# Attention's second pass: causal masks as POOL selects on the exponentials in place of mask matmuls

## The reference

```python
x_proj = x @ Wqkv + bqkv
q = x_proj[:, :, :C].reshape(B, n_head, T, hd)      # n_head 16, hd 16
k = x_proj[:, :, C:2 * C].reshape(B, n_head, T, hd)
v = x_proj[:, :, 2 * C:].reshape(B, n_head, T, hd)
att = jnp.einsum('bhtd,bhsd->bhts', q, k) * (1.0 / jnp.sqrt(jnp.float32(hd)))
causal = jnp.tril(jnp.ones((T, T), dtype=bool))
att = jnp.where(causal, att, jnp.float32(-jnp.inf))
att = jax.nn.softmax(att, axis=-1)
y = att @ v
y = jnp.transpose(y, (0, 2, 1, 3)).reshape(B, T, C)
return y @ Wproj + bproj
```

## Time and profile before

| | us |
|---|---|
| three runs | 4186.95, 4191.31, 4209.79 (median 4191.31) |
| profiled execution | 4200.33 |
| its span, first to last instruction | 4198.4 |
| PE busy in the span | 3853.1 (92%) |
| DVE busy | 2985.4 (71%) |
| ACT busy | 2260.1 (54%) |
| POOL busy | 1380.0 (33%) |

### The profile page before, as it was taken

How to read it: one execution, slowest core, us unless ns; L and a number is a source line. 1 busy time by engine, 2 the same in 40 slices (tenths; PEclk the granted TensorE clock), 3 DMA queues, 4 the chain that set the end, 5 groups by cost and what they waited for, 6 DMA issues and landing times. The chain is left out here.

```text
span 4198.4 us, 81224 instructions
## 1 busy us (share of the span) xinstructions
PE 3853.1 (92%) x28814; PEld 2524.3 (60%) x28814; DVE 2985.4 (71%) x7504; ACT 2260.1 (54%) x4454; POOL 1380.0 (33%) x1724
## 2 busy tenths in 40 slices
PE   4997899997579999999999999999999996899997
PEld 4886666664345555555555555555555553667664
DVE  6997457575467777777777777777777773467575
ACT  0110466664156656666666666666666664465664
POOL 2332133332524334243333334334343320132332
PEclk8999899999689999999999999999999998899999
DMA  1332112111767677766767766777676741112111
GB/s 57 100 100 94 42 46 65 52 56 38 136 93 116 104 99 112 106 109 100 120 99 107 118 103 105 107 117 102 101 117 99 107 67 47 41 57 64 41 56 46
DMA packets 701475, 361.54 MB, mean 86 GB/s; under 512 B 305072, under 2 KB 668080, under 8 KB 701104
## 3 DMA queue, kind: packets, MB, share of 16 engines
q1 hardware_dynamic: 701104, 356.65, 47.2%
HBM read 204.49 MB, written 150.99 MB: 85 GB/s over the span
## 5 line engine op out<-in xcount | busy, mean ns | idle before, releaser
L1591 DVE TENSOR_REDUCE att_maxima<-att_s 128x1 f32<-128x512 f32 (+3 forms) x3072 | 1521.6, 549 | 434.0 <-PE att_s L1770 217.2
L1691 ACT ACTIVATE att_probs<-att_s 128x512 f32<-128x512 f32 (+1 forms) x2560 | 1330.6, 556 | 869.9 <-PE att_s L1770 511.5
L1824 PE MATMUL att_s<-att_qs,att_ks 49*128 49x512 f32 (+3 forms) x3072 | 999.2, 401 | 89.6 <-DVE att_maxima L1591 42.2
L1800 PE MATMUL att_s<-att_ks,att_qs 48*128 48x512 f32 (+3 forms) x3072 | 993.6, 408 | 20.9 <-POOL att_ks L1464 13.4
L1824 PEld LDWEIGHTS att_s<-att_qs,att_ks 49*128 49x128 f32 x3072 | 473.9, 186 | 647.5 <-ACT att_probs L1691 403.4
L1852 PE MATMUL att_o_ps<-att_probs,att_vs 128*32 128x512 f32 (+3 forms) x6144 | 632.8, 498 | 1.9 <-issue 1.1
L1770 PE MATMUL att_s<-att_mask,att_places 64*128 64x64 bf16 (+1 forms) x5632 | 590.9, 209 | 0.6 <-issue 0.6
L1800 PEld LDWEIGHTS att_s<-att_ks,att_qs 48*128 48x128 f32 x3072 | 502.3, 188 | 36.2 <-issue 16.5
L1057 PE MATMUL ffn_h2p<-ffn_h,ffn_w 128*128 128x512 f32 x768 | 366.2, 599 | 2.8 <-ACT ffn_h L938 0.7
L1770 PEld LDWEIGHTS att_s<-att_mask,att_places 64*128 64x128 bf16 x5632 | 284.1, 96 | 112.4 <-issue 43.3
L1509 POOL TENSOR_TENSOR att_x_res<-att_x_res,att_bp_row 128x512 f32<-128x512 f32 x64 | 81.3, 1283 | 748.2 <-DMA att_x_res<-x 746.7
(11 more groups left out here) (238 smaller groups left out, 5809.3 us busy)
## 6 DMA issues: line engine op xcount, KB each, us to landing
att_staged<-qk_scratch SPq DMA_DIRECT2D x768, 128.0 KB, 7.1
qk_scratch<-att_parts SPq DMA_DIRECT2D x128, 512.0 KB, 3.1
ffn_x<-x SPq DMA_DIRECT2D x64, 512.0 KB, 5.2
ssm_x<-in_L_attn_a_x_dram SPq DMA_DIRECT2D x32, 512.0 KB, 3.9
x<-ssm_y SPq DMA_DIRECT2D x32, 512.0 KB, 2.9
x<-ffn_y SPq DMA_DIRECT2D x32, 512.0 KB, 3.1
att_x<-x SPq DMA_DIRECT2D x32, 512.0 KB, 12.7
v_scratch<-att_v_tok SPq DMA_DIRECT2D x32, 512.0 KB, 3.4
```

The lines of the kernel that those rows point to most:

```text
L1591: last = v.tensor_reduce(maxima_of[p][:, g, blk, 1 if t0 else 0:2 if t0 else 1], s1_ps[(2 * unit + 1 - g) % 3][:, col:col + w], AX.X, ALU.max)
L1691: a(probs[u % 2][2 * g + p][:, 0:n], bank[:, 0:n], ACT.Exp).then_inc(exp_done, 1)
L1800: last = mm(bank[:, col:col + w], rows_of(qs[buf], g, KROWS, p, BT * blk, BT * (blk + 1)), rows_of(ks[buf], g, KROWS, p, t0, t1), start=k ...
L1824: last = mm(bank[:, col:col + w], rows_of(ks[buf], g, SHIFT + 1, p, BT * j, BT * (j + 1)), rows_of(qs[buf], g, SHIFT + 1, p, t0, t1), star ...
```

## The change

The second pass's scores are no longer masked by matmuls. After the exponentials of a step of a unit with diagonal blocks POOL sets what lies under the diagonal to zero by `affine_select`, in place in `probs`, for both row groups in one instruction (so `probs` becomes one tile of 128 x 4 x 512 per unit parity). A new semaphore `cut` counts these steps; `times_v` of these six units waits for it behind its wait for the exponentials. The first pass's masks stay. POOL's other tasks move: the four casts from step 10 to 7, 8.6, 9.9 and 11.2 one by one, the two biases from 4 to 6, the normalisation from one piece at 8 to its powers and first quarter at 13 and further quarters at 14.7, 15.7 and 16.7. The selects stand at 2u + p + 0.5. The carrier instruction in `normalise` goes.

```diff
@@ -1170,11 +1170,13 @@
              [(0, 32, 64)], [(1, 32, 64)], [(2, 32, 64)], [(3, 32, 64)], [(4, 32, 64)],
              [(5, 40, 64), (7, 56, 64)], [(6, 48, 64)]]
     FIRST_U2, LAST_U2 = (0, 3), (2, 9)
+    ON_DIAGONAL = [u for u, unit in enumerate(PASS2) if any(t0 == BT * j for j, t0, _ in unit)]
     UNITS1, UNITS2 = 2 * len(PASS1), len(PASS2)
     STEPS = 2 * UNITS2
     LEAD = 4
     EVACUATE_AT = (7, 1)
-    LAY_OUT_AT, PREPARE_AT, PIECES = 10, 6, 2
+    LAY_OUT_AT, PREPARE_AT, PIECES = (7, 8.6, 9.9, 11.2), 6, 2
+    BIAS_AT, NORMALISE_AT = 6, (13, 14.7, 15.7, 16.7)
 
     X_PROLOGUE = 22
 
@@ -1228,7 +1230,7 @@
         qs = [sb(f"qs{k}", [P, HD * QT], F32R) for k in range(4)]
         ks = [sb(f"ks{k}", [P, HD * QT], F32R) for k in range(4)]
         vs = [sb(f"vs{s}", [P, CH * HD // P, 32]) for s in range(2)]
-        probs = [[sb(f"probs{k}_{i}", [P, CH]) for i in range(4)] for k in range(2)]
+        probs = [sb(f"probs{k}", [P, 4, CH]) for k in range(2)]
         o_sb = sb("o", [P, 2, CH])
         y_sb = sb("y", [P, KT, L // P, P])
         yT = [sb(f"yT{k}", [P, KT, 2 * P]) for k in range(2)]
@@ -1439,32 +1441,44 @@
                 g.memset(minus_half[:, :], -0.5).then_inc(mask_zero, 1)
                 g.memset(staged[0][:, :, :], 0.0).then_inc(const_ready, 1)
                 g.memset(staged[1][:, :, :], -1.0).then_inc(const_ready, 1)
-                def normalise(hb, s):
+                def rstds(hb):
                     pool.wait_ge(moments_done, hb + 1)
                     g.tensor_tensor(var_eps[:, :], moments[:, :, 1], eps[:, :], ALU.add).then_inc(eps_added, 1)
                     pool.wait_ge(eps_added, hb + 1)
                     g.tensor_tensor(rstd[:, :], var_eps[:, :], minus_half[:, :], ALU.pow).then_inc(rstd_ready, 1)
-                    pool.wait_ge(rstd_ready, hb + 1)
-                    g.tensor_tensor(pool_carrier[:, 2:3], eps[0:1, 0:1], eps[0:1, 0:1], ALU.add)
+
+                def normalise(hb, s, t):
+                    if t == 0:
+                        pool.wait_ge(rstd_ready, hb + 1)
+                    last = g.tensor_scalar(xt[s][:, t, :], xt[s][:, t, :], moments[:, t, 0:1], rstd[:, t:t + 1],
+                                           ALU.subtract, ALU.mult)
+                    if t == TT - 1:
+                        last.then_inc(xn_ready, 1)
+
+                def prepared(hb, s):
+                    rstds(hb)
                     for t in range(TT):
-                        last = g.tensor_scalar(xt[s][:, t, :], xt[s][:, t, :], moments[:, t, 0:1], rstd[:, t:t + 1],
-                                               ALU.subtract, ALU.mult)
-                    last.then_inc(xn_ready, 1)
-
-                def lay_out(quad, side, old):
-
-                    stack = (qs, ks)[side][quad % 4 if isinstance(quad, int) else lay_out.buf]
-                    pool.wait_ge(side_staged[side], 16 * N_STACK * (quad + 1))
-                    if old:
-
-                        pool.wait_ge(s2_full, 2 * STEPS * (quad - 3))
-                    g.tensor_tensor(pool_carrier[:, side:side + 1], eps[0:1, 0:1], eps[0:1, 0:1], ALU.add)
+                        normalise(hb, s, t)
+
+                def lay_out(quad, side, e, old):
+
+                    stack = (qs, ks)[side][quad % 4]
+                    if e == 0:
+                        pool.wait_ge(side_staged[side], 16 * N_STACK * (quad + 1))
+                        if old:
+
+                            pool.wait_ge(s2_full, 2 * STEPS * (quad - 3))
+                        g.tensor_tensor(pool_carrier[:, side:side + 1], eps[0:1, 0:1], eps[0:1, 0:1], ALU.add)
                     n = QT // PIECES
+                    last = g.tensor_copy(
+                        stack[0:ROWS, :].rearrange("p (t c) -> p t c", c=HD)[:, e * n:(e + 1) * n, :],
+                        staged[side][0:ROWS, :, e * n:(e + 1) * n].rearrange("p c t -> p t c"))
+                    if e == PIECES - 1:
+                        last.then_inc(laid_out[side], 1)
+
+                def lay_out_all(quad, side):
                     for e in range(PIECES):
-                        last = g.tensor_copy(
-                            stack[0:ROWS, :].rearrange("p (t c) -> p t c", c=HD)[:, e * n:(e + 1) * n, :],
-                            staged[side][0:ROWS, :, e * n:(e + 1) * n].rearrange("p c t -> p t c"))
-                    last.then_inc(laid_out[side], 1)
+                        lay_out(quad, side, e, False)
 
                 def make_masks():
                     for m in (places[:, :, :], mask[:, :, :, :]):
@@ -1496,6 +1510,21 @@
                         drawn(g.memset(places[row, 0, GROUP:P], 1.0))
                         drawn(g.memset(places[row, 3, 0:GROUP], 1.0))
 
+                def cut_probs(quad, step):
+
+                    u, p = step // 2, step % 2
+                    cols, col = [], 0
+                    for j, t0, t1 in PASS2[u]:
+                        if t0 == BT * j:
+                            cols.append(col)
+                        col += HD * (t1 - t0)
+                    pool.wait_ge(exp_done, 2 * STEPS * quad + 2 * step + 2)
+                    for col in cols:
+                        m = probs[u % 2][:, p::2, col:col + P]
+                        last = g.affine_select(out=m, in_=m, pattern=[[0, 2], [1, P]], compare_op=ALU.is_ge, fill=0.0,
+                                               base=0, channel_multiplier=-1)
+                    last.then_inc(cut, 1)
+
                 def v_bias(hb, e, index):
                     if index < X_PROLOGUE:
                         pool.wait_ge(v_free, 2 * hb + e + 1)
@@ -1511,19 +1540,23 @@
 
                 def slot(b, q):
                     first, more, more2 = flags(b)
-                    tasks = []
+                    quad = 4 * b + q
+                    tasks = [(u * 2 + p + 0.5, lambda step=2 * u + p: cut_probs(quad, step))
+                             for u in ON_DIAGONAL for p in range(2)]
                     for n, (at, kind, which) in enumerate(x_events(q, first, more, more2)):
                         if kind == "project" and which >= 6:
                             tasks += [(at + 3, lambda e=which - 6, n=n: v_bias(projected(b, q)[0], e, x_base(b, q) + n))]
                     if q < 2 and not first:
-                        tasks += [(4, lambda r=r: bias(b - 1, r)) for r in (2 * q, 2 * q + 1)]
+                        tasks += [(BIAS_AT, lambda r=2 * q + k: bias(b - 1, r)) for k in range(2)]
                     if q in (0, 2) and (more, None, more2)[q]:
-                        tasks += [(PREPARE_AT + 2, lambda: normalise(*((2 * b + 3, 1), None, (2 * b + 4, 0))[q]))]
+                        hb, s = ((2 * b + 3, 1), None, (2 * b + 4, 0))[q]
+                        tasks += [(NORMALISE_AT[0], lambda: rstds(hb))]
+                        tasks += [(NORMALISE_AT[t], lambda t=t: normalise(hb, s, t)) for t in range(TT)]
                     if more or q == 0:
-                        def turn(side):
-                            lay_out.buf = (q + 3) % 4
-                            lay_out(4 * b + q + 3, side, not first or q > 0)
-                        tasks += [(LAY_OUT_AT, lambda side=side: turn(side)) for side in range(2)]
+                        for side in range(2):
+                            for e in range(PIECES):
+                                tasks += [(LAY_OUT_AT[PIECES * side + e],
+                                           lambda side=side, e=e: lay_out(quad + 3, side, e, not first or q > 0))]
                     in_order(tasks)
 
                 def sequence(b):
@@ -1531,19 +1564,19 @@
                         slot(b, q)
 
                 pool.wait_ge(mask_zero, 2)
-                normalise(0, 0)
-                normalise(1, 1)
+                prepared(0, 0)
+                prepared(1, 1)
                 make_masks()
                 pool.wait_ge(loaded, 16 * len(loads))
                 for hb in range(2):
                     for side in range(2):
-                        lay_out(2 * hb, side, False)
+                        lay_out_all(2 * hb, side)
                     for e in range(2):
                         v_bias(hb, e, 8 * hb + 6 + e)
                     if hb == 0:
-                        normalise(2, 0)
+                        prepared(2, 0)
                         for side in range(2):
-                            lay_out(1, side, False)
+                            lay_out_all(1, side)
                 run(pool, sequence)
                 for r in range(4):
                     bias(NB - 1, r)
@@ -1688,7 +1721,7 @@
                         act.wait_ge(pv_done, UNITS2 * quad + u - 1)
                     n = sum(HD * (t1 - t0) for _, t0, t1 in PASS2[u])
                     bank = s2_ps[s2_use(q, step, g) % 3]
-                    a(probs[u % 2][2 * g + p][:, 0:n], bank[:, 0:n], ACT.Exp).then_inc(exp_done, 1)
+                    a(probs[u % 2][:, 2 * g + p, 0:n], bank[:, 0:n], ACT.Exp).then_inc(exp_done, 1)
 
```

(12 more changed lines are left out.)

## The result

| | before | after |
|---|---|---|
| median of four runs, us | 4192.71 (4186.95 to 4209.79) | 4270.75 (4240.60 to 4287.61) |
| ratio | | 1.0169 [1.0139, 1.0199] |
| profiled execution, us | 4200.33 | 4240.60 |
| its span, us | 4198.4 | 4238.7 |
| mean granted clock of PE over the span | 0.963 | 0.943 |

The forecast was 4169, the range 4140 to 4206. The quotient of the two medians is 1.0186, inside the ratio's interval.

A forecast was written before the change was run, and what follows sets the result against it. PE was taken to bound the kernel, busy 483 of 500 us in attention. Per batch entry -2.96 + 0.43 + 1.15 = -1.4 us, x 16 = -22 us, gives 4178 for the profiled execution, 4169 for the median; range 4140 to 4206.

The forecast's parts named there:

- What goes from PE: Second-pass mask matmuls, 3072 in all, leave PE: 0.72 us a slot in q = 0 and 2, 0.76 in 1 and 3.
- The select: POOL's select of 128 x 256, 16 a slot: taken at 0.42 us, bounds 0.41 and 1.224, range 0.41 to 0.545.
- (b): The select costs about 0.52 us: 1.4 us back per entry, nothing left, 4191; chance 0.17.
- (c): Select at 1.224 us delays the product with v of units 1 and 8: 13 us more per entry, 4370; chance 0.09.
- the rule of the Trainium skill: Compare-and-select bodies on POOL take 2.03 cycles an element, 1.03 if unrolled by two: 0.516 or 0.41 us a select.
- Where PE is late: Product with v at step 19 waits for POOL's selects: 1.15 us late in q = 2, 0.43 in q = 0.
- POOL is on time at step 16: In q = 0 POOL reaches step 16's selects without delay, so PE is only 0.43 us late; hangs on the residual's landing.
- rival (d): Moved casts or the residual's landing push POOL's chain in q = 0 later, by a microsecond an entry: 4185 to 4200; chance 0.06.
- The other checks: No select wait in steps 1, 3, 5 or 7 and none in q = 1; slots q = 1 and 3 shorter by 0.7 us.
- the sum: Per batch entry -2.96 + 0.43 + 1.15 = -1.4 us, x 16 = -22 us over the kernel.
- the four rivals: POOL keeps up and all of 2.96 us comes, 4144, chance 0.2; the others are (b), (c) and rival (d).

The follow-up runs named there:

- the filler: A POOL memset of about 0.5 us between two selects in q = 2, added to the kernel with both masks and selects: 4303.76 us, 1.0233.

## Why the prediction was wrong

- **What goes from PE: right in kind, too small.** 2.96 us an entry forecast, 3.8 measured with nothing in its place. Per slot 0.8 to 1.1 in place of 0.72 to 0.76: also stretches that I had at nothing or at 0.02 give a little.
- **The select: right.** 409 ns, 1024 of them; rivals (b) and (c), which needed 0.52 and more, are out. By the rule of the Trainium skill (GPSIMD Engine Reference, Performance pitfalls for Q7 kernels) that was weighed there, the lower of its two figures is the one that the chip shows.
- **Where PE is late: right for q = 2, too small for q = 0.** At step 19 the product is 0.96 us later than its normal 0.56 in q = 2 (forecast 1.15) and 0.86 later in q = 0 (forecast 0.43). In q = 0 step 17's product waits too, in 7 of 12 entries and for up to 2.4 us from its scores: the step that failed there is "POOL is on time at step 16", which I had said hangs on the residual. In all q = 0 loses 1.6 to 1.8 us where I had 0.43; that is a part of rival (d), about 20 us.
- **The other checks held.** No product waits long in steps 1, 3 and 7; in step 5 of q = 1 PE does come to the select just as it ends, and no time is lost. q = 1 is shorter by 0.9 us, q = 3, where its clock is whole, by 0.8 (forecast 0.76).
- **The step that failed: the sum.** It priced the late product of q = 2 at its length, 1.15 us, and took PE's clock behind it as it was in the rows read, 1.00. In the runs a wait of 0.9 us at this place has the clock at one half behind it in 7 of 14 entries, and each time costs up to 11.8 us (48.60 against 36.78). This put q = 3 at +3.5 us an entry where I had -0.76, 51 us of the 60 between the forecast and the trace over these 12 entries. The wait removed in two ways brings it back (1.0001 and 0.9959 in place of 1.0169), the wait made longer on PE's full work brings it forth (1.0233), the wait moved to q = 0 moves it to q = 1.
- **None of the four rivals was this.** Rival (c) was on the right side, with the wrong mechanism, and its 13 us an entry doesn't come out of its own terms: 8 for q = 0 and 2, and 3 or 6 for q = 1 and 3, as "each" is read. Rival (b)'s 1.4 ns an element is L713's; the casts of the earlier trace rows, 1.96 us on 1024 elements, show 1.9. What a wait of the bound engine does to its clock wasn't among the unknown costs, though the whole-run clock of the kernel before, 0.963, showed that its clock does fall at times.

Taken together: had the clock held, the change would have had about 3.8 less 1.1 (q = 2) and 1.7 (q = 0), 1 us an entry, some 16 us; my 22 was near that by two errors that cancel.

Three things stay open. What decides in which entries the clock falls (7 of 14 behind the same wait, nearly every second one) no run here shows. Nor does any show why 0.8 us at step 19 of q = 0 has a slower clock behind it in one of 10 entries of the change, and in none of 7 with the early normalisation in q = 2 alone, where 0.9 us at step 19 of q = 2 has it in half. And the holes of up to 2 us in PE's order with nothing waited for, which cost the kernel with both masks and selects its q = 1, have no cause in these profiles.

## What to carry to other kernels

Work taken off the bound engine is worth having only where it doesn't wait anyway; leave it there elsewhere, and move it only where its new engine has room in every slot, not on average. Price a wait of TensorE twice: by its length, and by what its clock does behind it at that place. One late product a batch entry, by a microsecond, took back here more than 3072 matmuls had cost. Look at the spread over the slots and at the granted clock of each before the mean: a slot of 36.8 us that sometimes takes 48.6 is one cause, and its place names it.

## What was unexpected of the hardware

PE's granted clock fell from 1.00 to 0.50, its lower level of 1.2 GHz, behind idles of 0.9 to 1.04 us at step 19 of q = 2 in stretches where PE was busy 4.67 of 6 us, and stayed there for 14 to 41 us, once for 3.4, while PE was busy (in the one shown, all the time). It did so in 7 of 14 entries of the change and 6 of 14 with the filler. Idle of 0.60 at the same place with more matmuls around it brought none in 14 entries; idle of 0.8 at the same step of q = 0 brought one of 3.4 us in 10; longer idle at step 17 of q = 0 (2.99 us in the row shown) brought 34 to 38 us of it in eight. The Trainium skill (TensorE: Matmul & The Clock Gate, Part 1) tells of the same two levels and of a fall after the engine has been idle; the trace agrees on the levels, but at step 19 of q = 2 PE was never idle for more than a fraction of the time around the fall, and came back to the upper level only long after it was busy again.

Behind step 19 of q = 3, where PE waits for no select, 14 to 17 us at the lower level followed in none or one of the 15 entries before the last where the kernel had all its mask matmuls, in five with no masks at all, in one to five where selects stood for them, and in one when units 0, 8 and 9 had theirs back. Matmuls that cost no time bought 0.7% (0.9930 [0.9900, 0.9959] to 0.9859 [0.9832, 0.9885]).
